# Graph network kernel on one core: the order of the first slot load and the weight loads in each MoE round

## The reference

```python
h = x @ W_in + b_in
for l in range(L):                       # L = 3
    agg = segment_sum(h[src], dst) / deg
    logits = concatenate([h, agg]) @ router_W[l] + router_b[l]
    vals, idx = top_k(logits, 2); gates = softmax(vals)
    weak = relu(agg @ weak_W[l, e] + weak_b[l, e])
    strong = relu(agg @ strong_W1[l, e] + strong_b1[l, e]) @ strong_W2[l, e] + strong_b2[l, e]
    moe = sum over e of gate[e] * experts[e]
    h = h + sigmoid(h @ conf_W[l] + conf_b[l]) * moe
out = h @ W_out + b_out
```

## Time and profile before

| | |
|---|---|
| median of three executions | 6334.04 us (6332.07, 6334.04, 6337.51) |
| span of the profiled execution | 6337.4 us, against 6337.51 us for the longest of the three times |
| PE busy | 3244.1 us (51%) |
| DVE busy | 3183.0 us (50%) |
| ACT busy | 1224.2 us (19%) |
| POOL busy | 4748.6 us (75%) |
| gathers of rounds 0 to 2 | 2400, from 389 us to 3966 us |
| gathers of rounds 3 and 4 | 1600, from 4147 us to 6262 us |

### The profile page before, as it was taken

How to read it: one execution, slowest core, us unless ns; L and a number is a source line. 1 busy time by engine, 2 the same in 40 slices (tenths; PEclk the granted TensorE clock), 3 DMA queues, 4 the chain that set the end, 5 groups by cost and what they waited for, 6 DMA issues and landing times. The chain is left out here.

```text
span 6337.4 us, 56993 instructions
## 1 busy us (share of the span) xinstructions
PE 3244.1 (51%) x11612; PEld 1941.8 (31%) x11612; DVE 3183.0 (50%) x6341; ACT 1224.2 (19%) x2737; POOL 4748.6 (75%) x4528
## 2 busy tenths in 40 slices
PE   6219789898478798965798999700000000000000
PEld 4105455455245454543455655500000000000000
DVE  4225455553345455524454555445655645566563
ACT  1003223233123232322233333300000000000000
POOL 6767777777677777757777777577777777777777
PEclk9559899999799899987899999955555555555555
DMA  2143333332333333333333333122222222222221
GB/s 72 35 127 93 95 93 93 94 94 91 111 95 93 94 92 93 93 107 97 93 93 92 93 94 94 38 53 55 55 56 56 55 53 52 55 55 55 55 55 50
DMA packets 229707, 494.53 MB, mean 78 GB/s; under 512 B 96471, under 2 KB 113038, under 8 KB 229486
## 3 DMA queue, kind: packets, MB, share of 16 engines
q0 software_dynamic: 184432, 463.70, 27.2%
q1 hardware_dynamic: 45188, 29.87, 1.6%
HBM read 462.21 MB, written 31.05 MB: 78 GB/s over the span
## 5 line engine op out<-in xcount | busy, mean ns | idle before, releaser
L544 POOL DMA_INDIRECT ring<-hidden_tab,stage x2400 | 2628.8, 1095 | 798.1 <-issue 582.6
L544 POOL DMA_INDIRECT ring<-gat_tab,stage x1600 | 1550.8, 969 | 497.5 <-issue 448.9
L827 DVE TENSOR_TENSOR x_res<-x_res,ring 128x1024 f32<-128x1024 f32 x450 | 551.3, 1225 | 546.3 <-POOLq L555 440.7
L1581 PE MATMUL ps_w1a<-agg_team_t,wbuf 128*128 128x512 f32 (+1 forms) x1248 | 561.2, 572 | 4.8 <-ACT strong L1278 4.1
L1604 PE MATMUL ps_gate<-wbuf,strong 128*128 128x256 f32 x2400 | 559.9, 379 | 0.0
L1581 PE MATMUL ps_w1b<-agg_team_t,wbuf 128*128 128x512 f32 (+1 forms) x1248 | 556.0, 568 | 0.0
L1698 PE MATMUL ps_w1a<-ident,agg_team_t 128*128 128x128 f32 x28 | 7.8, 434 | 1045.6 <-DVE agg_team_t L1151 1045.6
L1604 PE MATMUL ps_wide<-wbuf,strong 128*128 128x256 f32 x2304 | 537.2, 379 | 0.0
L1604 PEld LDWEIGHTS ps_gate<-wbuf,strong 128*128 128x128 f32 x2400 | 432.6, 190 | 99.7 <-issue 35.8
L1604 PEld LDWEIGHTS ps_wide<-wbuf,strong 128*128 128x128 f32 x2304 | 415.3, 190 | 78.5
L1416 ACT ACTIVATE ps_gate<-shifted 128x36 f32<-128x36 f32 x296 | 60.4, 204 | 1959.3 <-DVEq L1062 1951.6
(11 more groups left out here) (334 smaller groups left out, 4684.5 us busy)
## 6 DMA issues: line engine op xcount, KB each, us to landing
ring<-hidden_tab,stage POOLq DMA_INDIRECT x2400, 2.8
ring<-gat_tab,stage POOLq DMA_INDIRECT x1600, 2.5
hidden_tab<-h_res SPq DMA_DIRECT2D x12, 512.0 KB, 3.0
wbuf<-in_L_gnn_strong_W SPq DMA_DIRECT2D x6, 1024.0 KB, 7.9
wbuf<-in_L_gnn_strong_W SPq DMA_DIRECT2D x12, 512.0 KB, 10.0
wbuf<-in_L_gnn_weak_W SPq DMA_DIRECT2D x6, 512.0 KB, 5.4
stage<-slot_tab SPq DMA_DIRECT2D x125, 16.0 KB
slot_tab<-wbuf SPq DMA_DIRECT2D x1, 1584.0 KB, 6.3
```

The costliest lines, as they stand in the source:

```text
L544: return pool.indirect_dma_start(out=ring[:, b, 0:width], out_offset=None, in_=table, in_offset=bass.IndirectOffsetOnAxis(ap=stage[:, half ...
L827: nc.vector.tensor_tensor(wide_s, wide_s, rows(u), ALU.add).then_inc(ring_free, 1)
L1581: last = mm(ps_w1[c % 2][:, 0:size * P], w1_w[:, k, s, c * P:(c + 1) * P], agg_team_t[:, k, 0:size * P], start=k == 0, stop=k == 1)
```

## The change

In each round SP now first waits for `round_gathered` (from round 1 on) and loads the first 32 columns into `stage[:, 0, :]`. Only then does it issue the eight weight loads, and these now wait also for `arrived >= bodies * UNITS * r + r + 1`. In round 0 they also stand behind the wait for the second store of `slot_tab` (`s_slotst_rest`). The loop of further loads is the same.

```diff
             for r in range(LAYERS + 2):
+                if r:
+                    sp.wait_ge(round_gathered, r)
+                def load(m, half):
+                    return sp.dma_start(stage[:, half, :], slot_tab[:, bass.ds(m * RING, RING)]).then_inc(staged[half], 16)
+
+                def next_load(m, half):
...
+                sp.dma_start(stage[:, 0, :], slot_tab[:, 0:RING]).then_inc(staged[0], 16)
+                if r == 0:
+                    sp.wait_ge(s_slotst_rest, 16)
                 if r < LAYERS:
 
+                    sp.wait_ge(arrived, bodies * (UNITS * r) + (r + 1))
                     if r:
                         sp.wait_ge(w2_ready, r * BATCHES * 2 * NS)
                     for k in range(2):
...
-                if r:
-                    sp.wait_ge(round_gathered, r)
...
-                sp.dma_start(stage[:, 0, :], slot_tab[:, 0:RING]).then_inc(staged[0], 16)
-                if r == 0:
-                    sp.wait_ge(s_slotst_rest, 16)
                 with sp.Fori(1, bodies // 2 + 1) as j:
                     next_load(j * 2, 1)
                     next_load(j * 2 + 1, 0)
```

More of the change, by code:

```diff
@@ L390, in _ @@
             for r in range(LAYERS + 2):
-                if r < LAYERS:
-                    if r:
[L394 to L402, removed]
                 if r:
@@ L420, in _ @@
                     sp.wait_ge(s_slotst_rest, 16)
+                if r < LAYERS:
+                    sp.wait_ge(arrived, bodies * (UNITS * r) + (r + 1))
+                    if r:
+                        sp.wait_ge(w2_ready, r * BATCHES * 2 * NS)
+                    for k in range(2):
+                        sp.dma_start(wk_w[:, k, :].rearrange("p (e n) -> p e n", e=NW),
+                                     weak_W[r, :, k * P:(k + 1) * P, :].rearrange("e p n -> p e n")).then_inc(s_wts, 16)
+                        sp.dma_start(w1_w[:, k, :, :],
+                                     strong_W1[r, :, k * P:(k + 1) * P, :].rearrange("s p n -> p s n")).then_inc(s_wts, 16)
+                    for c in range(4):
+                        sp.dma_start(w2_w[:, c, :, :],
+                                     strong_W2[r, :, c * P:(c + 1) * P, :].rearrange("s p n -> p s n")).then_inc(s_wts, 16)
                 with sp.Fori(1, bodies // 2 + 1) as j:
```

## The result

The changed kernel takes 6313.35 us (median of five, 6308.55 to 6317.53) against 6334.04 us for the kernel before (median of five, 6332.07 to 6340.71). The ratio is 0.9962, with a 95% interval from 0.9950 to 0.9974: 0.38% faster, 20.7 us by the medians. The forecast was 6317.5, in a range from 6297 to 6331.

What follows compares the result with a forecast made beforehand. POOL's gathers were taken to lead each MoE round, standing still between rounds for the slot load. Earlier starts of 40.3 us less 24 us of stalls gave -16.3 us: 6317.5 us, range 6297 to 6331.

Steps and rivals of the forecast that it cites:

- What bounds the kernel: MoE rounds: POOL leads to each round's end, held only by its own pace, landings it waits for costing 0.3 us.
- Earlier starts: First gathers of rounds 0, 1 and 2 come 14.4, 13.0 and 12.9 us earlier, 40.3 us in all.
- no row of over a microsecond would be left for `stage<-slot_tab`: Sign in POOL's list of waits: the wait for the slot load, 57.5 us before, should be gone.
- When the weights go: SP's first weight load in a round is issued 0.7 us after the first gather, at the third gather's count.
- The landing: A gather issued among the weights lands after 6.9 us: 2.8 undisturbed plus 4.1 from the table write.
- turn-taking by single packets: DMA engines: each of a gather's 48 packets lets one weight packet pass, 0.16 us and no stall.
- 9 to 17 descriptors a turn: DMA engines: longer turns delay a gather by 1.4 to 2.7 us, with stalls of 1.3 to 2.6 us.
- The stalls: POOL stalls 4.0 us ahead of the seventh and eleventh gather of rounds 0 to 2, 24 us in all.
- Covers: Weights land near T0 (first gather's start) + 20, needed at T0 + 71.2; the second slot load's lateness also costs nothing.
- B: Rival: gathers among the weights are hardly delayed; net gain 25 to 40 us, 6294 to 6309 us; chance 0.24.
- C: Rival: gathers held until weights are through, seventh at T0 (first gather's start) + 18.9; 6327 to 6330 us; chance 0.26.
- D: Rival: weights run at half rate while gathers stay locked out; +32 us, 6366 us; chance 0.04.

Runs made afterwards that it cites:

- before_fourth: The kernel before, with POOL's wait for the preceding unit at the fourth gather instead of the third in the MoE rounds: 6323.34 us, ratio 0.9983.
- weights_later: The changed kernel with the weights held for four more units, some 20 us later in each round: 6310.32 us, ratio 0.9965.
- stage_only: The changed kernel without the weights' new wait for `arrived`; the slot load still goes ahead of them: 6310.53 us, ratio 0.9965.
- reuse_weights: The changed kernel, but rounds 1 and 2 load no weights and compute with those of layer 0: 6300.44 us, ratio 0.9947.

## Why the prediction was right

The mechanism came as forecast: the early starts, the delayed landings, two stalls a round and their places. The net gain of 16.3 us was short of the measured 20.7, in the main because the stalls were priced too high.

- **What bounds the kernel.** POOL led to the end of each round: the earlier start less the stalls came out at the end of the span, 22.0 against 21.8 us. "Nothing but its own pace holds it" was not quite right. The waits that the earlier trace rows shows cost 0.3 us a time, but before_fourth found 10 us in longer ones, which the profile calls "issue" and those rows leave out.
- **Earlier starts.** 13.0 and 12.9 us were forecast for rounds 1 and 2, and 13.0 and 12.8 came. Round 0 gave 16.3 instead of 14.4. SP's load went out 1.6 us earlier, which is the spread of the preparation between executions and luck for the profiled gain, and the first gather followed 2.55 us after it, where 2.8 had been taken. POOL was ready in time. That no row of over a microsecond would be left for `stage<-slot_tab` was a wrong sign: round 0's 11.9 us stayed, as the forecast's own times imply (POOL free at 362.5, the load not issued until 371.9).
- **When the weights go.** The first weight load is issued 0.53 and 0.55 us after the first gather in rounds 0 and 1 (0.7 forecast), that is with the third gather's count and not after four have arrived.
- **The landing.** 6.9 us was forecast from the one table write among the weights. The six gathers that POOL waited for took 6.4, 6.3, 6.0, 6.2, 7.1 and 6.1 us, 6.3 on average; others took up to 8.6. The row was nearer than the turn-taking by single packets of the Trainium skill ("DMA: Bandwidth & Descriptors", "Queues, rings and completion order"), 0.16 us. The estimate with its 9 to 17 descriptors a turn, 1.4 to 2.7 us, was also too small: the six landed 3.2 to 4.3 us late.
- **The stalls.** Two a round, at the seventh and eleventh gather, as forecast. Two terms were sized too high. The landing was 6.3 us on average and not 6.9, which makes 3.3 us over six stalls. The restart was taken as 0.9 us, and in every one of the six the waiting gather starts 0.76 or 0.77 us after the landing (383.01 and 383.77 in round 0), which makes 0.8. So the six stalls cost 20.1 us and not 24. With the 1.9 us by which round 0 started earlier than forecast this is about the 5.5 us by which the forecast sum, 16.3, fell short of the span's 21.8.
- **Covers.** The weights' and the second slot load's lateness cost nothing visible. The last weights landed 20.9 to 22.6 us after the first gather of their round, a little after the forecast 20. PE's first team of round 1 came 77 us after it, with a wait that had shrunk by just the earlier start less the stalls, from 86.4 to 79.6 us, and weights_later held the weights back over 20 us more without loss. The row of that wait:

```profile
1670.34 1.94 PE L1552 MATMUL ps_wide<-ident,x_res 128*128 128x128 f32 x8 [79.58 <-DVE x_res L843]
```

- **Rivals.** B (hardly a delay) falls by the landings of 6.0 to 7.1 us. C (gathers locked out) would have put the seventh gather at T0 + 18.9; it came at T0 + 11.0, 10.6 and 11.7, some 10 us ahead of the weights' last landing. D had two conditions. The weights did slow down, from 16.3 to 16.8 us between the first issue and the last landing to 20.3 to 22.1, but the gathers were not locked out meanwhile.

## What to carry to other kernels

A small load that the next stage waits for should be issued ahead of bulk loads on the same queue, when the bulk is needed much later; here that alone was the whole gain. Bulk that must run beside small DMAs whose landings are waited for is best cut into pieces that are through before the next one is issued, each tied to the progress of the small ones, so that the delay falls on one that nobody is waiting for yet: 0.5 MB a piece cost 1.7 us in three rounds, 5 MB at once 20 us. A wait on small DMAs should stand as late as its consumers allow, since its slack is what absorbs a slower landing; here DVE could take its sums a gather later, because POOL led. And a list of waits can hide a wait under "issue": look at the timeline for gaps that always stand at the same place of a loop.

## What the runs showed of the hardware

- An indirect DMA of 128 rows of 1 KB beside the full load of weights landed late: the table write after 6.5 us instead of 2.4, the gathers that POOL waited for in the changed kernel after 6.0 to 7.1 us instead of 2.8, and the slowest gather after 8.6. With little left to come the delay is smaller: in stage_only, rounds 1 and 2, whose last weights land 9 us after the first gather, the first four gathers took 5.3 to 5.8 us and the fifth 4.4. The longest landing of round 1 is 3.3 us without weights, 4.4 behind 0.5 MB and 5.2 behind 1 MB. What inside the DMA engines holds this amount of work ahead of a newcomer was not measured.
- Where POOL waited for a landing in the loop, the next indirect DMA started 0.76 or 0.77 us after it, in all six stalls of the changed kernel. With an undisturbed landing of 2.8 us that leaves 0.2 us of slack against the three gathers in between (3.78 us).
- The first gather behind each stall of the changed kernel takes 1.52 to 1.55 us instead of 0.95. The stall is not the reason: in the kernel before the 11th gather of round 1 takes 1.54 us behind a gap of 0.47, and in reuse_weights 1.53 behind 0.44. DVE begins its sum over the unit that has just landed at about the same moment; that the two hinder each other was not tested.
- One of the six executions of weights_later took 13,271.87 us, while the other five lay between 6306.78 and 6311.36. Nothing here explains it, and it is not counted in the ratio.
